# Self attention in a decoder kernel: global query rows moved ahead on VectorE, two masks moved behind the shift's rows, and TensorE's turn of the shift moved behind both global value products

## The reference, cut to what matters

```
x: (16, 256, 128)          H = 16 heads of D = 8, blocks of 64 rows, 8 global rows
mask = same block | global query row | global key column
q, k, v = layernorm(x) @ Wq + bq, ... @ Wk + bk, ... @ Wv + bv
attn = softmax(where(mask, q k^T / sqrt(8), -inf))
x = x + (attn @ v) @ Wo + bo
x = x + cross_attention(layernorm(x), ctx)
x = x + experts(layernorm(x)) + shared_expert(layernorm(x))
```

## Time and profile before

| | |
|---|---|
| median of 3 runs | 580.83 us (580.59 to 580.95) |
| the profiled execution: its own time, its span | 579.96 us, 577.8 us |
| busy shares of the span | PE 83%, PEld 63%, DVE 73%, ACT 51%, POOL 51% |
| granted TensorE clock, mean | 0.955 |

### The profile page before, as it was taken

How to read it: one execution, slowest core, us unless ns; L and a number is a source line. 1 busy time by engine, 2 the same in 40 slices (tenths; PEclk the granted TensorE clock), 3 DMA queues, 4 the chain that set the end, 5 groups by cost and what they waited for, 6 DMA issues and landing times. The chain is left out here.

```text
span 577.8 us, 16568 instructions
## 1 busy us (share of the span) xinstructions
PE 481.1 (83%) x5675; PEld 363.3 (63%) x5675; DVE 420.3 (73%) x1308; ACT 297.2 (51%) x756; POOL 293.1 (51%) x540
## 2 busy tenths in 40 slices
PE   1968988888888888859999999999777999999700
PEld 1856666666666666546767677676645788888600
DVE  7658989999788888867999899888572444344237
ACT  2636566555555566524665646565432544444337
POOL 4743444433333333210357878777772477777720
PEclk9979999999999999987999999999989999999765
DMA  6526444455354465415233333332024333333149
GB/s 190 110 56 124 66 65 61 81 115 112 100 107 100 103 107 101 102 41 142 62 82 83 96 91 79 93 81 80 32 77 130 101 116 115 114 114 93 56 159 301
DMA packets 96002, 58.30 MB, mean 101 GB/s; under 512 B 24560, under 2 KB 92224, under 8 KB 95920
## 3 DMA queue, kind: packets, MB, share of 16 engines
q1 hardware_dynamic: 74016, 39.80, 29.6%
q10 hardware_dynamic: 17328, 7.54, 6.3%
q0 software_dynamic: 4576, 9.91, 5.1%
HBM read 20.83 MB, written 17.50 MB: 66 GB/s over the span
## 5 line engine op out<-in xcount | busy, mean ns | idle before, releaser
L730 DVE TENSOR_REDUCE nmax<-ps 128x8 f32<-128x512 f32 x128 | 85.3, 682 | 19.1 <-PE ps L1559 15.2
L627 POOL DMA_INDIRECT expert_out<-ey,xt x79 | 75.9, 961 | 41.0 <-DVE ey L1121 20.8
L485 POOL TENSOR_SCALAR veps<-mv 128x2 f32<-128x2 f32 x48 | 11.4, 237 | 163.5 <-issue 117.8
L1252 ACT ACTIVATE probs<-ps 128x512 f32<-128x512 f32 x128 | 73.5, 602 | 7.9 <-PE ps L1764 5.7
L574 POOL DMA_INDIRECT expert_in<-xn,sloti x64 | 65.6, 1025 | 17.6 <-issue 17.6
L1116 DVE TENSOR_TENSOR eh<-ps,sg 128x256 f32<-128x256 f32 x40 | 17.0, 425 | 56.4 <-ACT sg L1450 56.4
L1962 PE MATMUL ps<-wgu,turned 128*128 x160 | 41.3, 380 | 0.3 <-ACT turned L1444 0.3
L1559 PE MATMUL ps<-kbd,qs 96*64 96x128 bf16 x512 | 38.0, 293 | 2.4 <-DMA kbd<-part 1.9
L487 POOL TENSOR_TENSOR rstd<-veps,minus_half 128x2 f32<-128x2 f32 x48 | 36.7, 764 | 4.0
L1444 ACT COPY turned<-ps 128x512 f32<-128x512 f32 (+1 forms) x43 | 23.8, 555 | 25.2 <-PE ps L1955 22.0
L671 DVE TENSOR_SCALAR xn<-x_rows,mv,rstd 128x128 f32<-128x128 f32 x64 | 24.9, 429 | 15.1 <-POOL rstd L487 14.9
(11 more groups left out here) (242 smaller groups left out, 1346.9 us busy)
## 6 DMA issues: line engine op xcount, KB each, us to landing
qs<-part ACTq DMA_DIRECT2D x96, 64.0 KB
kbd<-part SPq DMA_DIRECT2D x192, 32.0 KB
xt<-expert_in SPq DMA_DIRECT2D x80, 72.0 KB
ck_scr<-wgu SPq DMA_DIRECT2D x6, 512.0 KB, 3.6
qs<-part SPq DMA_DIRECT2D x48, 64.0 KB
ckbd<-ck_scr SPq DMA_DIRECT2D x16, 192.0 KB, 2.9
kbd<-part SPq DMA_DIRECT2D x48, 64.0 KB
wgu<-in_L_ffn_gate_up_w SPq DMA_DIRECT2D x4, 512.0 KB, 3.8
```

Of the source, the lines that this page charges most:

```text
L627: pool.indirect_dma_start(ys, bass.IndirectOffsetOnAxis(xt[p][:, E:E + 1].bitcast(I32), 0), ey[q % 4][:, j, :], None).then_inc(e_(f"out{q ...
L730: v.tensor_reduce(nmax[:, u, 8 * half:8 * half + 8], bank[:, :].rearrange("p (h k) -> p h k", k=64), AX.X, ALU.max, negate=True).then_inc( ...
L1252: a_.activation(probs[:, 2 * i:2 * i + 2, :], P2[i % 2][:, :].rearrange("p (j q) -> p j q", j=2), ACT.Exp, scale=SCALE).then_inc(s("probs" ...
```

## The change

On DVE, `global_rows(b - 1)` moves from behind `global_query_max(b)` to right behind `attended(b - 1)`. `self_vg(b + 1)` and `global_heads_out(b)` move behind `shift_rows`; in the last sequence's iteration (b = 15) the latter keeps its place. On TensorE, `turn_shift(b + 1)` moves from between the two global value products to behind both. No instruction is added or taken away.

```diff
@@ VectorE, self_body
                 if has(b - 1):
                     attended(b - 1)
+                    global_rows(b - 1)
                 if b == 0:
                     self_last_part(1)
                 if has(b):
                     global_query_max(b)
-                if has(b - 1):
-                    global_rows(b - 1)
...
-                if has(b):
+                if b + 1 == B:
                     global_heads_out(b)
                 self_maxima(b + 1, 1, 0)
                 self_maxima(b + 1, 1, 1)
                 if has(b + 1):
-                    self_vg(b + 1, 1 - p)
                     whole_max(b + 1)
                     shift_rows(s_, b + 1, 1 - p)
+                    self_vg(b + 1, 1 - p)
+                    if has(b):
+                        global_heads_out(b)
                     if has(b + 2):
                         self_last_part(b + 2)
@@ TensorE, global_values_out
                 mm(OD[:, 0:S], vg[p][:, 0, :], probs_g[:, :], start=False, stop=True, skip_group_check=True)
+                mm(OD[:, S:2 * S], vg[p][:, 1, :], probs_g[:, :], start=False, stop=True, skip_group_check=True).then_inc(s_("od"), 1)
                 if has(b + 1):
                     turn_shift(s_, b + 1)
-                mm(OD[:, S:2 * S], vg[p][:, 1, :], probs_g[:, :], start=False, stop=True, skip_group_check=True).then_inc(s_("od"), 1)
```

## The result

The changed kernel took 583.74 us (582.85 to 585.23, 4 runs) against 580.71 us of the kernel before (4 runs): a ratio of 1.0065, 95% interval 1.0035 to 1.0095. It is slower, by well under 1%, and its time lies above the range. A second comparison, further down, gave 1.009 (1.0062 to 1.0117). The span of the profiled execution went from 577.8 to 580.8 us.

The account below looks back on a forecast made before the run. It took a closed chain through VectorE, TensorE and ScalarE, 13.05 us per iteration, as the bound, plus a two-iteration transfer chain. Gains of 0.72 + 0.64 = 1.4 us from 580.83 gave 579.4 us, range 577.1 to 582.7.

Parts of the forecast that it names:

- The chain of the kernel before: Closed chain of 13.05 us: division, maximum, rows, output projection, turn, ScalarE's copy and projections, subtraction, spread; TensorE unwaiting from projection to turn.
- Rows ahead of the maximum: VectorE: global rows done 0.38 us earlier, maximum 0.57 and ScalarE's exponent 0.53 later; chain gains 0.16, or 0.06 without overlap.
- ScalarE's queue: Work queued behind the late exponent, not TensorE's turn (6.86), releases copy L1299, at 7.11 to 7.21 instead of 7.27 us.
- the rival in which the full 0.38 comes: ScalarE's queue absorbs the late maximum; chain gains 0.38 us, 3.2 us in all, total 577.6; chance 0.17.
- I cost it at nothing: VectorE's reciprocal L805, at most 5.59 instead of 5.06 us, costs nothing, except up to 0.2 in the one VectorE-filled iteration.
- The slower rival: Late maximum delays exponent, reciprocal, copy L1299, cast, subtraction and transfers; 582.7 us if L1299 is 0.2 late, worst 585.3; chance 0.20.
- L1299 still released by TensorE (then the gain is larger): Sign in the changed profile that the forecast is wrong: ScalarE's copy still waits for TensorE's turn, with a larger gain.
- the queue's upper bound: Latest release of ScalarE's copy L1299 by its own queue: 6.68 plus 0.53, that is 7.21 us behind L742.
- They cost 0.20 each ... 3.46 stays: VectorE's two masks cost 0.20 us each in either place; L738 ends 0.40 earlier, subtraction to spread stays 3.46.
- The turn behind both products: TensorE: second product (0.54 us) slides into the 0.81 wait before the turn; worth nothing while L742 doesn't move.
- The sum over transfers: Of 14 iterations one gains nothing, nine with late transfers 0.08 us each, four 0.16; together 1.4 us.
- the halving: In nine iterations with late transfers the cast's gain is spread over two iterations, 0.08 us each instead of 0.16.

## Why the prediction was wrong, step by step

**The chain of the kernel before** had a link missing. Its length, 13.05, and the links named (the rows, the output projection, the turn, ScalarE's copy, the subtraction) are right, but between the output projection and the turn the prediction saw TensorE work "without a wait between". There the chain leaves TensorE: VectorE's addition waits for the output projection (0.16), and the next projection waits for the addition, since `self_project` waits for `x_new`; the output projection and the next projection share the bank A0. The addition ends at 5.77 and L1535 starts at 5.92, 0.15 later, as in the changed kernel and in every iteration of the kernel before. There was no margin at all; the wait did not show only because the product ahead was still running.

**Rows ahead of the maximum.** Half right. TensorE was given 0.31 rather than 0.38: the rows start 0.11 behind L760, not 0.04, because L799 had filled that gap too. The maximum came 0.64 late, where 0.54 was costed. But the turn could not follow the 0.31, because the addition stands between: even with the reciprocal out of the way it starts at 5.28, and the turn is 0.07 earlier, not 0.38. So ScalarE's queue was not what held the gain, and the rival in which the full 0.38 comes would have failed as well.

**"I cost it at nothing", of the reciprocal, is the step that failed first.** Its own time was right: at most 5.59 forecast, 5.46 measured. What queued behind it was named, the addition and the layer norm, but who waits for the addition was not asked. It delayed the projection by 0.19 and turned a gain of 0.07 (12.98, shown with the reciprocal behind) into a loss of 0.20 (13.25). The slower rival, which had been given 0.20, has the copy L1299 late by 0.2, and it was (7.47 in place of 7.27), but by TensorE's turn and not by ScalarE's queue as that rival has it. The sign "L1299 still released by TensorE (then the gain is larger)" came true with a loss. The time of 7.21 in the kernel with the reciprocal behind meets the queue's upper bound by luck, as shown above.

**"They cost 0.20 each ... 3.46 stays" is the second.** The distance of starts of an instruction is its cost only if what follows could have taken its place. L793 needs L730's result and starts 0.10 to 0.12 behind its end with or without L771 between. L810 did cost 0.20 before and costs it after; L771 cost nothing before and 0.20 after. Rows 3 showed it: L730 ends at 130.88, L793 starts at 130.99.

**The turn behind both products:** right, worth nothing (13.06).

**The sum over transfers** is open. The steps grew by 0.39, and of 14 x 0.39 = 5.5 us the first comparison shows 3.0 and the second 5.2. That late transfers took the rest in the first fits its waits (1.2 us in place of 3.9), but no run isolates it, and the halving is not confirmed.

## What to carry to other kernels

When an instruction moves on an engine that runs its list in order, list who waits for each instruction behind it, fences of shared buffers included, even where the profile of before shows no wait. A wait that ends while the engine is still busy with the instruction ahead doesn't show. What tells is the distance from the end of the input's writer to the start: if it is the same in every iteration and every version (here 0.15 us from the addition to the projection), that writer is the releaser. Before costing a move between two dependent instructions at its distance of starts, take the hole into account: the successor's start behind its own input's end tells whether the mover was free there. And read a change of 0.2 us per iteration from the undisturbed step, which repeats to 0.02 us, not from totals that vary by several us. Then check the whole too: here a shorter step did not bring a shorter time that could be told, except once.

## What the runs showed of the hardware

In these traces a VectorE instruction that needs the result of the one ahead started 0.10 behind that one's end (changed kernel: L730's end at 157.95 to L793 at 158.05). An independent one started about 0.08 ahead of it (L810 put in L771's place: L730's end at 156.58 to L810 at 156.50). Between the two lies a free place of nearly 0.2 us, which held a 128x128 multiplication for nothing: from L730 to L793 it is 1.39 with and without it. The Trainium skill, VectorE: DVE Perf Modes, says in its rules for kernel authors that for chained operations the DRAIN, the emptying of the pipeline behind an operation, happens regardless. The trace doesn't show the DRAIN by itself; it agrees in so far as the dependent L793 starts only 0.10 behind its input's end, and it shows beside it that an independent instruction between the two does not add to that.

TensorE's projection started 0.15 behind the end of the VectorE addition whose bank it writes, in all but one of the 182 cases in the fourteen traces, and in undisturbed iterations ScalarE's copy started 0.42 behind the start of the two products of TensorE that it reads, whether or not the profile shows a wait ahead of them.
